# Attention variances on four groups of output rows, and a last stage cut into halves of eight pairs

## The reference, cut to what matters

```python
def _layer_norm(t, g, b, eps=1e-05):
    mu = t.mean(-1, keepdims=True)
    var = ((t - mu) ** 2).mean(-1, keepdims=True)
    return (t - mu) * jax.lax.rsqrt(var + eps) * g + b
...
skip = xin + _layer_norm(om, ln1_g, ln1_b)
ffn = jax.nn.gelu(skip @ ffn_w1 + ffn_b1, approximate=False) @ ffn_w2 + ffn_b2
out = skip + _layer_norm(ffn, ln2_g, ln2_b)
```

## Time and profile before

| | |
|---|---|
| median of 3 runs | 788.99 us (788.33 to 789.17) |
| profiled execution | 790.13 us |
| its span | 788.3 us |
| PE busy | 673.9 us (85%) |
| PE weight loads | 366.2 us (46%) |
| DVE busy | 510.6 us (65%) |
| ACT busy | 485.4 us (62%) |
| POOL busy | 354.6 us (45%) |
| HBM read, written | 20.71 MB, 9.37 MB |

### The profile page before, as it was taken

How to read it: one execution, slowest core, us unless ns; L and a number is a source line. 1 busy time by engine, 2 the same in 40 slices (tenths; PEclk the granted TensorE clock), 3 DMA queues, 4 the chain that set the end, 5 groups by cost and what they waited for, 6 DMA issues and landing times. The chain is left out here.

```text
span 788.3 us, 20928 instructions
## 1 busy us (share of the span) xinstructions
PE 673.9 (85%) x8456; PEld 366.2 (46%) x8456; DVE 510.6 (65%) x989; ACT 485.4 (62%) x963; POOL 354.6 (45%) x441
## 2 busy tenths in 40 slices
PE   3795789999999999999999659999999998749780
PEld 2572455555555545555555323333333366735350
DVE  4794477777777787777778421578778786371181
ACT  3655266777777777777776548877777756624000
POOL 4687446778777777787776530022211223100000
PEclk9667599999999999999999969999999999969955
DMA  9550000000000000000000020121122120020268
GB/s 212 137 126 11 1 2 3 2 2 3 2 3 3 2 3 3 2 3 2 3 2 3 2 56 1 27 55 41 41 54 54 47 62 2 28 74 2 63 191 266
DMA packets 15718, 31.42 MB, mean 40 GB/s; under 512 B 7488, under 2 KB 9284, under 8 KB 15620
## 3 DMA queue, kind: packets, MB, share of 16 engines
q1 hardware_dynamic: 12592, 29.16, 13.7%
q10 hardware_dynamic: 2760, 0.66, 0.5%
q0 software_dynamic: 272, 0.27, 0.2%
HBM read 20.71 MB, written 9.37 MB: 38 GB/s over the span
## 5 line engine op out<-in xcount | busy, mean ns | idle before, releaser
L785 POOL TENSOR_TENSOR sc<-sc,mx 128x512 f32<-128x512 f32 x128 | 133.7, 1044 | 107.7 <-DVE mx L719 107.7
L716 DVE TENSOR_TENSOR sc<-s_ps,bias_tab 128x512 f32<-128x512 f32 x128 | 87.6, 684 | 57.7 <-PE s_ps L527 57.7
L1415 POOL TENSOR_TENSOR square<-xs 128x1024 f32<-128x1024 f32 x16 | 34.1, 2134 | 164.0 <-DVE xs L1157 164.0
L538 PE MATMUL t_ps<-consts,sc 128*128 128x128 f32 x512 | 84.9, 289 | 15.8 <-ACT pt L650 12.5
L538 PEld LDWEIGHTS t_ps<-consts,sc 128*128 128x128 f32 x512 | 54.6, 142 | 90.9 <-issue 55.2
L650 ACT ACTIVATE pt<-t_ps 128x512 f32<-128x512 f32 x128 | 75.5, 590 | 30.5 <-PE t_ps L538 29.4
L719 DVE TENSOR_REDUCE mx<-sc 128x8 f32<-128x512 f32 x128 | 87.8, 686 | 4.4
L1072 ACT ACTIVATE hs<-h_ps,fb1s 128x512 f32<-128x512 f32 x128 | 78.1, 689 | 17.7 <-PE h_ps L981 17.5
L527 PE MATMUL s_ps<-kx,qu 32*64 32x128 f32 x2048 | 72.3, 278 | 3.5 <-DVE kx L740 2.9
L981 PE MATMUL h_ps<-xs,fw 64*128 64x512 f32 x256 | 66.9, 634 | 1.3 <-ACT hs L1072 1.2
L527 PEld LDWEIGHTS s_ps<-kx,qu 32*64 32x64 f32 x2048 | 56.7, 134 | 15.2 <-issue 13.4
(11 more groups left out here) (205 smaller groups left out, 1298.4 us busy)
## 6 DMA issues: line engine op xcount, KB each, us to landing
raw<-in_x_dram SPq DMA_DIRECT2D x32, 256.0 KB, 4.7
xr<-in_x_dram SPq DMA_DIRECT2D x32, 256.0 KB, 3.9
out_dram<-x SPq DMA_DIRECT2D x32, 256.0 KB, 4.1
rec_scratch<-r SPq DMA_DIRECT2D x4, 224.0 KB, 2.5
w<-in_L_conv_W_dram SPq DMA_DIRECT2D x1, 784.0 KB
w<-in_L_conv_W_dram SPq DMA_DIRECT2D x1, 672.0 KB
xs<-rec_scratch SPq DMA_DIRECT2D x16, 28.0 KB
xs<-rec_scratch ACTq DMA_DIRECT2D x16, 28.0 KB
```

The costliest lines, as they stand in the source:

```text
L538: last = pe.transpose(t_ps[:, m], sc[n % KEPT][:, m].rearrange("c h k -> c (h k)"), ident)
L716: dve.tensor_tensor(sc[n % KEPT][:, :, :, :], s_ps[j][:, :, :, :], bias_tab[:, j, hp], ALU.add)\
L785: pool.tensor_tensor(v, v, mx[n % KEPT][:, :].unsqueeze(2).broadcast_to([128, 8, TOK]), ALU.subtract)\
```

## The change

In attention `variances` makes four matmuls of 256 columns, one for each half of each `csq`, on four groups of 32 output rows, in place of two of 512 on two. `rv` becomes 128 partitions x 256, so ACT's logarithm and exponential work on 128x256 instead of 64x512. `spread_rstd` makes four matmuls of 64 rows and 256 columns with a new matrix `spread_half`, filled by eight small DVE operations in `bias_table`.

In the last stage everything from the score copy to the loads back is done for pairs 0 to 7 and then for pairs 8 to 15. DVE's chain of 13 links runs twice, at half width; the second run stands between the feature copies of the first half. `r` is zeroed by ACT (an activation with scale 0) and no longer by POOL. The transposed `st` goes into the free part of bank 1 and is copied by DVE and ACT. The first layer works on 256 columns with two banks in turn, and the transposes of the second half's picks stand between its parts. The return of half 0 (writes and all 16 loads) is on SP's queue, that of half 1 on ACT's; each k has its own semaphore. The two mixings of k = 0 stand between the pieces of half 1's first layer, the rest after its second layer. The banks of mixing are chosen by `MIX_SETS`.

```diff
-            rv = sb(stage, "rv", [C, COLS])
+            rv = sb(stage, "rv", [128, COLS // 2])
+            spread_half = sb(stage, "spread_half", [128, 2, 128])
...
-                    for j in range(2):
-                        last = pe.matmul(n_ps[rows(j), :], mean_rows, csq[j][:, :], start=True, stop=True)
+                    for g in range(4):
+                        half = slice(256 * (g % 2), 256 * (g % 2 + 1))
+                        last = pe.matmul(n_ps[rows(g), 0:256], mean_rows, csq[g // 2][:, half], start=True, stop=True)
...
-                    for j in range(2):
-                        last = pe.matmul(spread_bank(p, j), spread_image[rows(j)], rv[rows(j), :], start=True, stop=True)
+                    for h in range(2):
+                        for j, (lo, hi) in enumerate(HALVES):
+                            last = pe.matmul(spread_bank(p, j)[:, 256 * h:256 * (h + 1)], spread_half[lo:hi, h], rv[lo:hi, :],
+                                             start=True, stop=True)
...
-                    act.activation(rv[:, :], n_ps[0:C, :], ACT.Ln, bias=eps[0:C, 0:1]).then_inc(s["var_ln"], 1)
+                    act.activation(rv[:, :], n_ps[:, 0:256], ACT.Ln, bias=eps[:, 0:1]).then_inc(s["var_ln"], 1)
...
+                for g in range(4):
+                    dve.memset(spread_half[rows(g), 1 - g % 2], 0.0)
+                    dve.tensor_copy(spread_half[rows(g), g % 2], spread_image[rows(g)])
                 dve.wait_ge(bias_in, 32)
...
+            def send_back(eng, h):
+
+                for i in range(2):
+                    t = ROW_TILES[2 * h + i]
+                    eng.wait_ge(s["rec"], 2 * h + i + 1)
+                    eng.dma_start(rec_dram[128 * t:128 * (t + 1), :], rec[:, t]).then_inc(rec_out[h], 16)
                 eng.wait_ge(rec_out[h], 32)
+                for k in range(2):
+                    for a in range(2):
+                        rows = rec_dram[256 * a + 128 * h:256 * a + 128 * (h + 1)]
+                        for q in range(4):
...
+                            eng.dma_start(dst[:, k], src[:, k]).then_inc(rec_in[2 * h + k], 16)
+
+            MIX_BANKS = ((4, 5, 6, 7), (0, 1, 2, 3))
+            MIX_SETS = (0, 0, 1, 0, 1, 0, 1, 0)
...
-                    for t in range(2):
-                        last = pool.memset(r[:, t], 0.0)
...
+                    shares(1)
+                    take_picks(0)
+                    best(1)
+                    compare(1)
+                    take_feat(0)
+                    collect(1)
+                    take_feat(1)
+                    rank(1)
+                    take_feat(2)
+                    place_by_rank(1)
+                    assert links[0] == 2 * N_PICK
+                    take_feat(3)
+                    take_picks(1)
+                    take_rec(0)
+                    for n in range(4, 8):
+                        take_feat(n)
+                    add(0)
+                    add(1)
+                    take_rec(1)
+                    for u in range(2, 8):
+                        add(u)
...
+                    for t in range(2):
+                        act.activation(r[:, t].rearrange("c (g n) x -> c g (n x)", n=4),
+                                       ident.unsqueeze(1).broadcast_to([128, 16, 128]), ACT.Copy, scale=0.0)\
+                           .then_inc(s["r_zero"], 1)
...
+                    turn_back(3)
+                    first_layer(0, (0, 1))
+                    turn_picks(1)
+                    first_layer(0, (2, 3))
+                    second_layer(0)
+                    gather(4)
...
+                    first_layer(1, (0, 1))
+                    mix(0)
+                    first_layer(1, (2, 3))
+                    mix(1)
+                    second_layer(1)
+                    for u in range(2, 8):
+                        mix(u)
```

More of the change, by code:

```diff
@@ new lines, in _, with tiles, shares @@
+                    full = [128, 2, TOK]
+                    def tiles(h):
+                        return range(2 * h, 2 * h + 2), slice(2 * h, 2 * h + 2)
+                    def shares(h):
+                        _, at = tiles(h)
+                        dve.wait_ge(s["exped"], h + 1)
+                        link(dve.tensor_reduce(esum[:, at], e[:, at, :], X, ALU.add))
+                        link(dve.reciprocal(esum[:, at], esum[:, at]))
+                        link(dve.tensor_tensor(pr[:, at, :], e[:, at, :], esum[:, at].unsqueeze(2).broadcast_to(full), ALU.mult))
@@ new lines, in best, with compare @@
+                    def best(h):
+                        each, at = tiles(h)
+                        for t in each:
+                            last = dve.max(top[:, t], pr[:, t])
+                        link(last)
+                        for t in each:
+                            last = dve.max_index(tidx[:, t], top[:, t], pr[:, t])
+                        link(last)
+                        link(dve.tensor_copy(tidf[:, at, :], tidx[:, at, :]))
+                    def compare(h):
+                        _, at = tiles(h)
+                        for k in range(TOP):
+                            last = dve.tensor_tensor(sel[:, k, at], iota[:, :].unsqueeze(1).broadcast_to(full),
+                                                     tidf[:, at, k:k + 1].broadcast_to(full), ALU.is_equal)
+                        link(last)
@@ L1586, in _ @@
+                    own(0)
+                    own(1)
                     dve.memset(zeros[:, :], 0.0)
                     dve.wait_ge(iota_in, 16)
[L1588 to L1592 removed]
@@ L1639, in _ @@
[L1639 to L1644 removed]
+                    shares(0)
+                    best(0)
+                    compare(0)
+                    collect(0)
@@ new lines, in second_layer @@
+                    def second_layer(h):
+                        pe.wait_ge(s["hid"], 4 * (h + 1))
+                        pe.wait_ge(s["picked_a"], 4)
+                        pe.wait_ge(s["picked_b"], 4)
+                        pe.wait_ge(s["st_copied"], 4)
+                        after(pe, s["rec"], 2 * h)
+                        for i in range(2):
+                            t = ROW_TILES[2 * h + i]
+                            for m in range(4):
+                                last = pe.matmul(psb[i][:, 0:OUTDIM], hid[:, m, 128 * t:128 * (t + 1)], w2[:, m],
+                                                 start=(m == 0), stop=(m == 3))
+                            last.then_inc(s["rec_ps"], 1)
```

312 lines of the change are left out of this document (166 added, 146 removed).

## The result

The changed kernel takes **781.8 us** (median of 9 runs, 776.07 to 786.05) against 788.55 for the kernel before on the same chip (9 runs, 787.89 to 790.68): ratio 0.991 [0.989, 0.993]. It is faster by 6.7 us, where 15.2 was forecast, and lies 0.8 us above the range. Its profiled execution is itself one of 781.8 us, with a span of 780.0; before it was 790.13 and 788.3.

A forecast was written before the change was run, and what follows sets the result against it. The prediction took PE to bound attention, a chain of waits the last stage, and the stores' bandwidth its end. Gains of 7.1 us (attention) and 8.1 us (last stage), together 15.2, took 788.99 to 773.8 us; range 769 to 781.

The forecast's parts named there:

- steady part: Attention, pairs 0 to 12: PE sets the pace; cheaper variances and spreading save 0.37 us per pair, 4.8 us.
- the drain: Attention's last pairs, 14 and 15, a pure latency chain: variances and activations together gain 2.3 us.
- Rival (a): Attention: the split matmuls give nothing, as records or GpSimd's squares set the time; 4.8 us fall away, 778.6; chance 0.10.
- The eight small operations in `bias_table`: Start of attention: VectorE fills the new spreading matrix under cover, taken at nothing; without cover up to 3.4 us lost.
- half 0's chain: Last stage: VectorE's picks for the first half, at half width, take 7.6 us; gathers start 12.0 us into the stage.
- the stand before the first layer: Last stage: PE waits about 3 us for VectorE, whose second chain of picks delays half 0's features.
- The last bias add: Last stage: half 1's layers end at T 62.0 (us after the stage's start), with 1.7 us for a lowered clock.
- Half 1 returns through ScalarE's queue: Last stage: write 1.94, eight issues 2.66, landing 5.45 us, then 2.28 to the adds of pair 8 at T 74.3.
- the store stream behind it: End of the last stage: first store of the second half at T 77.4, then 16.35 us of stores, ending T 93.75.
- Rival (b): Last stage: half 1's loads starve beside the stores of pairs 4 to 7; 4.7 us lost, 778.5 us; chance 0.17.
- (c): Last stage, rival: PE's clock stays at 1.2 GHz through both layers; end 24.5 us later, 798.3 us; chance 0.04.
- (d): Last stage and attention, rival: halves do not overlap and attention gains little; within 1.6 us of before; chance 0.02.

The follow-up runs named there:

- attn_only: The kernel before with the attention edits alone, last stage as before: 784.89 us, ratio 0.9929 to the kernel before.
- after_again: The changed kernel measured once more, with no edit: 780.18 us, ratio 0.9888 to the kernel before.
- var_records: The changed kernel with each variance matmul cut once more, to eight of 128 columns (16 records): 777.36 us, one execution.
- hold0: The changed kernel with all stores held until half 1's loads have landed: 789.18 us, ratio 0.9975 to the kernel before.
- split_feat: The changed kernel with half 1's loads shared by SP's and ScalarE's queues and half 0's features taken before half 1's rank and placing: 771.47 us, ratio 0.9775.
- split: The changed kernel with half 1's loads shared by ScalarE's and SP's queues, ahead of the stores of pairs 4 to 7: 775.51 us, ratio 0.9825; repeated, 777.65 us.
- hold_k2: The changed kernel with the stores of pairs 4 to 7 held until half 1's first eight loads landed, loads on one queue: 782.56 us, ratio 0.9911.
- split_w: The changed kernel with half 1's loads shared by two queues and the stores of pairs 2 and 3 also behind them: 777.88 us, one execution.

## Why the prediction was wrong

- **Attention, right** in the steady part: variances 0.57 (0.58), spreading 1.07 (1.10), twelve periods 4.60 shorter (12 x 0.37 = 4.4). The rest, 2.6 (0.37 for pair 12 and 2.3 for the drain), agrees with the help of luck. The step from pair 13's to pair 14's variances, taken at nothing, is 1.5 us shorter in this profile (18.52 to 17.01), mostly because matmuls that took 1.11, 1.94 and 1.35 us took 0.66, 1.10 and 1.04; in attn_only and after_again it is 18.55 again. The activations gained 0.21 each (682 to 476 ns and 631 to 416), not 0.26. And the longer feed-forward stage, which no term had, took 1.4 back. Rival (a) is out, by var_records too. The eight small operations in `bias_table` do not stand out of the moving start of attention: 135.3 to 138.7 in the twelve profiles that have them, 136.7 and 136.4 in the two that do not. A cost of up to 1 us could hide there.
- **Picks, gathers and layers, nearly right**: half 0's chain ran 7.6 us (679.57 to 687.16), gathers started at T 11.9, the stand before the first layer was 3.33, which is the one foreseen as about 3. The last bias add ended at T 64.0 instead of 62.0. 1.0 of it is the later first layer, T 23.0 for 22; the rest is mostly that the low clock cost about 2.5 and not 1.7.
- **The step that failed** is "Half 1 returns through ScalarE's queue, where nothing is behind it: write 1.94, eight issues 2.66, landing 5.45". The first two are prices of a write and of issues (seven, not eight, in that chain) that ran without stores beside them. The queue was indeed empty, but the 16 DMA engines were not: the stores that the change had just made early ran beside it. It measured 5.67 for the write, 5.3 until the last issue that counted, 4.31 for the landing: 15.4 with the gaps for 10.05, so 5.3 of the 8.5 us by which the stage's end, T 102.2, missed the forecast T 93.75. The rest is the 2.0 above and 1.2 in the store stream behind it (20.7 from the adds of pair 8 to the end, for 19.45). The landing alone was priced with company. The prediction says one write of 224 KB ran beside it; SP's queue shows two:

```profile
745.01 1.49 SPq L1553 DMA_DIRECT2D rec_scratch<-r  x2
```

With no stores and no such writes it took 4.08 (hold0), and 4.31 in the changed kernel, so this term was 1.1 to 1.4 too high and hid part of the miss.
- **Rival (b) was the mechanism**, given 0.17, and priced too low at 4.7. It reckoned only the loads, against the stores of pairs 4 to 7. It left out that the write already meets the stores of pairs 0 to 3, and that the issues themselves slow down. It stood beside the forecast as an either-or, though the text already had both the stores' times (T 54 to 63, from T 66.6) and the return's (T 62 to 72), which overlap: the range should have followed from them. With (b) as the likeliest case the forecast was 778.5, and with the write and the issues priced too it would have come close to what was measured: 773.8 + 5.3 = 779.1.
- (c) did not happen: the clock was 1.00 through the second layers and half 1's first. (d) did not happen either; the halves overlap as written, and the first store is at T 57.9 (for 54).
- **Where the expected gain went**: 8.1 us were forecast for the last stage and -0.3 to 1.6 measured. Most of it turned into a wait for DMA. In split_feat, with its two further edits, the overlap is worth 10.6 us (101.9 to 91.3). It got there from the changed kernel's 102.2 by 6.1 in the return (15.4 to 9.3) and 4.9 before it (last bias add at T 64.0 and T 59.1).

What stays open is why the issue of a small DMA on one queue takes longer while another queue is storing; the runs show that it does and that it ends with the stores, not which resource it waits for. What moves the start of attention, and in three profiles the stretch behind it, was not tested either. Nor was the share of `split`'s gain that comes from letting the stores go at the issue of the loads instead of their landing.

## What to carry to other kernels

When a change starts a bulk stream earlier, price every small, latency-bound transfer that now runs beside it anew, its issue and its receipt included: a duration read while the stream was silent is no price. Here it paid to put the small transfers that the end waits for on two queues and ahead of the next bulk ones, and to let the bulk go again as soon as they were issued. And where one engine serves two chains, let it finish the piece another engine stands for first: a stand of 3.3 us was paid nearly twice, once as a wait and once in clock.

## What the runs showed of the hardware

- The issue of a small DMA (28 KB) on ScalarE's queue took 0.345 us in the median (at most 0.348) with no stores beside it (hold0, hold_k2), and 0.53, up to 1.20, beside stores of 256 KB on SP's queue (changed kernel).
- The write of the last rows landed in 1.9 to 2.2 us with none or only the first four stores just before it (kernel before, hold0, split_w) and in 4.1 to 5.7 with stores beside it.
- During a stand of 3.33 us of PE, after 4.58 us at full clock with PE busy 4.45, the granted clock fell (0.75 over the stand, 0.50 behind it); after one of 0.88 us it was 1.00.
- Four column groups side by side took sixteen records of 128 columns in the time of eight of 256: 0.58 and 0.57 us (var_records, changed kernel).
